# Batch 1's block sums of a pooling layer taken in two rounded passes, with the operands split by ScalarE and GpSimd

## The chip, the cores and the metric

The kernel runs on one core of one Trainium2 chip. The metric is the device time of one execution in microseconds (us). TensorE (PE), VectorE (DVE), ScalarE (ACT), GpSimd (POOL) and SyncE (SP, which issues the DMAs) each take their instructions in program order and wait for one another by semaphores. The program is written by hand, engine by engine, so the order in each of the five streams is the order in the code.

## The reference, cut to what matters

`x` is (2, 1024, 256) in float32. The first layer adds a mixture of eight experts and a shared expert; the second adds a masked softmax pooling over the 1024 positions of each batch:

```python
x = x + _L0_cond_ref(x, ...)             # gated experts, E=8, F=1024, and a shared one
# second layer, hidden = x, A = 64
attn_in = jnp.tanh(jnp.einsum('bsd,da->bsa', hidden, W1) + b1)
scores = jnp.einsum('bsa,a->bs', attn_in, v)
# the mask is l <= j, l >= j or l != j, by the batch's prompt type
masked_scores = jnp.where(mask, scores[:, None, :], -1e30)
p = jax.nn.softmax(masked_scores, axis=-1)
pooled = jnp.einsum('bjl,bld->bjd', p, hidden) / cnt[..., None]
x = x + pooled
```

## The kernel before

The first layer takes nearly all of the time: a loop of 144 groups in which TensorE multiplies split operands. A float32 tensor is split into a rounded part (type fp32r) and what is left (also fp32r), and three matmuls of the parts stand for one float32 matmul. The second layer of batch 0 is woven into the last groups of that loop. The second layer of batch 1, and the pooling of both batches, stand behind the loop, in about the last 27 us.

The pooling works on 8 blocks of 128 positions. Inside a block the masked softmax is a 128x128 matrix `probT` that multiplies the block's rows of `x1` (`pool_probs`, line 1380, plain float32). What a position takes from the other blocks goes through block sums: for each block j the sum of `exp(score - block maximum) * x1` over its 128 positions. `block_sums` (line 1361) makes these with one matrix `e_diag[b][:, j, :]` per block, which holds the weights of block j in column j and in copies of it at 32, 64 and 96, accumulated over the blocks in one PSUM bank, 258 columns wide. ScalarE rounds the sums (`copy_sum`, line 758), VectorE subtracts the rounded part (`rest_sum`, line 1113), and `pool_carries` (line 1388) multiplies them by the carried weights `carry_r` into the same bank as `pool_probs`. `finish` (lines 1122, 1125, 1128) divides and adds, one pair of blocks at a time, into `x_nat`, and SyncE stores each pair. There are four pairs in a batch and four PSUM banks for pooled blocks, so a bank is used again when `finish` has read it (`out_done`).

`e_diag` is made by VectorE in `block_weights`. For batch 0 it is fp32r: three instructions write the rounded weights (line 1097), one forms the rest `e_rest` (line 1102), one writes the rest at column 96 (line 1106). `x1` of batch 0 is split by GpSimd (`split_x1`, lines 617 and 621) while the loop still runs. For batch 1 `e_diag` is plain float32, written by one instruction (line 1091), and `block_sums(1, ...)` multiplies it by the unsplit `x1[1]` in float32.

The order behind the loop, where the change lies:

- TensorE: sums of batch 0, the first four pooled blocks of batch 0, `pick_maxima` (line 1325, batch 1's maxima spread over the lanes), three blocks of batch 1's sums, pooled blocks 4 and 5, the other five blocks of the sums, pooled blocks 6 and 7, then the four pairs of batch 1.
- VectorE: batch 1's maxima (up to line 1061), `block_weights(1)`, `finish` of pair 0, the two arguments of batch 1's exponentials (`prob_args`, line 1081), `finish` of pairs 1 and 2, `rest_sum(1)`, `finish` of pair 3, then `finish` of batch 1.
- ScalarE: the exponential of the block weights (line 754), the eight exponentials of the carried weights (line 770), `round_carry` (779), the exponentials of `probT` (785), with `copy_sum(1)` ahead of the last two.
- GpSimd: waits for `carry_rounded` and takes the rest of each half of `carry_r` (`rest_carry`, line 606).

Of the kernel before, what the change touches and what calls it, by code (L numbers as in the profile page):

```python
# [6 lines left out]
F32 = mybir.dt.float32  # L7
F32R = mybir.dt.float32r
# [5 lines left out]
P = 128  # L14
# [15 lines left out]
NP = 7  # L30


def cond_resid_kernel(nc, x, fside, shared_gate, prompt_type, Wg, Wu, Wd, Sg, Su, Sd, W1, b1, v, out):
# [64 lines left out]
    with ExitStack() as ctx:  # L98
# [4 lines left out]
        def place(name, shape, dt, offset):  # L103
            return nc.alloc_sbuf_tensor_at(name, shape, dt, offset=offset)
# [12 lines left out]
        def sem(name):  # L117
            return ctx.enter_context(nc.semaphore(name))
# [100 lines left out]
        for b in range(B):  # L219
            at = l1_at[b]  # L220
            probT.append(place(f"probT{b}", [P, NJ, P], F32, at))
            at += S * 4

            neg_max.append(place(f"neg_max{b}", [2 * LANE, NJ, P], F32R, at))
            carry_r.append(place(f"carry_r{b}", [P, S], F32R, at))
            at += S * 4
            e_diag.append(place(f"e_diag{b}", [P, NJ, P], F32 if b else F32R, at))
            at += S * 4
            attnT.append(place(f"attnT{b}", [P, BANK], F32, at))
            at += BANK * 4  # L230
            carry.append(place(f"carry{b}", [P, S], F32, at))
            at += S * 4

            for name, where in (("row", row), ("row_self", row_self), ("row_before", row_before),
                                ("row_after", row_after), ("neg", neg)):
                where.append(place(f"{name}{b}", [P, P], F32, at))
                at += P * 4
            neg_r.append(place(f"neg_r{b}", [2 * LANE, P], F32R, at))
            at += P * 4
            x1.append(place(f"x1_{b}", [P, NJ, XA], F32, at))  # L240
            assert at + NJ * XA * 4 <= l1_at[b] + 5 * S * 4 + (NJ * XA * 4 + 511) // 512 * 512 + S * 4


        x1_bytes = (NJ * XA * 4 + 511) // 512 * 512
        assert 2 * x1_bytes <= RAWS * PAIR * (8 * P + D) * 4
        x1_hi = place("x1_hi", [P, NJ, XA], F32R, raw_at)
        x1_lo = place("x1_lo", [P, NJ, XA], F32R, raw_at + x1_bytes)

# [54 lines left out]
        x1_done = sem("x1_done")  # L305
        x1_copied = sem("x1_copied")
        x1_ones = sem("x1_ones")
        x1_rounded = sem("x1_rounded")
        x1_split = sem("x1_split")
        col_done = sem("col_done")  # L310
        col_ready = sem("col_ready")
# [24 lines left out]
        def dve_steps(b, *names):  # L336
            for name in names:
                DVE_L1[name, b] = len(DVE_L1) + 1
# [2 lines left out]
        BLOCKS = ("blkmax", "diag", "before", "after")  # L341
        JOINS = ("bias", "max1", "max2")
        CARRIED = ("carg", "earg", "cmax")
        EDIAG = (("ediag0", "ediag32", "ediag64", "erest", "ediag96"), ("ediag",))
        MAXIMA = ("neg", "negr", "negl", "neg0", "neg1")
        dve_steps(0, *BLOCKS, *CARRIED, *JOINS, *MAXIMA[:4], "parg0", "neg1", "parg1", *EDIAG[0])
        dve_steps(1, *BLOCKS, *JOINS, *CARRIED, *MAXIMA[:3], *EDIAG[1])
        FINISHED = tuple(tuple(f"{n}{j}" for n in ("den", "rden")) for j in range(0, NJ, HEAD))
        dve_steps(0, *FINISHED[0])
        dve_steps(1, "parg0", "parg1")  # L350
        for names in FINISHED[1:]:
            dve_steps(0, *names)
        for names in FINISHED:
            dve_steps(1, *names)
# [101 lines left out]
        def _(pool):  # L456
# [145 lines left out]
            def rest_carry(b, n):  # L602

                half, rows = slice(n * BANK, (n + 1) * BANK), slice(LANES[2], LANES[2] + LANE)
                pool.wait_ge(carry_rounded, b * NT + n + 1)
                nc.gpsimd.tensor_tensor(carry_r[b][rows, half], carry[b][rows, half],
                                        carry_r[b][rows, half].bitcast(F32), ALU.subtract).then_inc(carry_done, 1)

            def split_x1():

                pool.wait_ge(gu_split, NU)
                pool.wait_ge(d_split, NU)
                pool.wait_ge(x1_copied, NB)
                pool.wait_ge(x1_ones, 1)
                for n in range(NB):
                    two = slice(n * JB, (n + 1) * JB)
                    nc.gpsimd.tensor_tensor(x1_hi[:, two, :], x1[0][:, two, :],
                                            zero[:, 0:1].unsqueeze(2).broadcast_to([P, JB, XA]),
                                            ALU.add).then_inc(x1_rounded, 1)
                    pool.wait_ge(x1_rounded, n + 1)  # L620
                    nc.gpsimd.tensor_tensor(x1_lo[:, two, :], x1[0][:, two, :], x1_hi[:, two, :].bitcast(F32),
                                            ALU.subtract).then_inc(x1_split, 1)

            for b in range(B):
                pool.wait_ge(p_done[3], end_of_b[b] + 1)
# [15 lines left out]
            for b in range(B):  # L641
                for n in range(NT):
                    if b * NT + n:
                        pool.wait_ge(carry_done, b * NT + n)
                    rest_carry(b, n)

        @block.scalar
        def _(act):
# [103 lines left out]
            def exp_blocks(b):  # L752
                act.wait_ge(dve_l1, DVE_L1["earg", b])
                nc.scalar.activation(e_blk[:, b, :], e_blk[:, b, :], ACT.Exp).then_inc(e_done, 1)
# [117 lines left out]
            copy_sum(0)  # L872
            copy_x1(1, 2, 3)
            exp_blocks(1)
            halves = [range(n * BANK // P, (n + 1) * BANK // P) for n in range(NT)]
            for blocks in halves:
                exp_carry(1, blocks)
# [8 lines left out]
        def _(dve):  # L886
# [121 lines left out]
            def after_step(name, b):  # L1008
                dve.wait_ge(dve_l1, DVE_L1[name, b])
# [75 lines left out]
            def block_weights(b):  # L1085
                dve.wait_ge(e_done, b + 1)
                dve.wait_ge(diag_zeroed, b + 1)
                e_all = e_blk[:, b, :].unsqueeze(2).broadcast_to([P, NJ, NJ])
                if b:
                    n = len(LANES) - 1  # L1090
                    step_done("ediag", b, nc.vector.tensor_tensor(
                        e_diag[b][:, :, 0:n * LANE].rearrange("p i (n j) -> p i n j", j=LANE)[:, :, :, 0:NJ],
                        e_all.unsqueeze(2).broadcast_to([P, NJ, n, NJ]), eye[:].unsqueeze(2).broadcast_to([P, NJ, n, NJ]),
                        ALU.mult))
                    return
                for at in LANES[:3]:
                    step_done(f"ediag{at}", b, nc.vector.tensor_tensor(e_diag[b][:, :, at:at + NJ], e_all, eye[:],
                                                                       ALU.mult))
                if b == 0:

                    after_step("ediag0", b)
                    step_done("erest", b, nc.vector.tensor_tensor(e_rest[:], e_all, e_diag[b][:, :, 0:NJ].bitcast(F32),
                                                                  ALU.subtract))
                    after_step("erest", b)
                    at = LANES[3]
                    step_done(f"ediag{at}", b, nc.vector.tensor_tensor(e_diag[b][:, :, at:at + NJ], e_rest[:], eye[:],
                                                                       ALU.mult))

            def rest_sum(b):

# [79 lines left out]
            carried_maxima(1)  # L1190
            negative_maxima(1)
            block_weights(1)
            finish(0, range(HEAD))
            for n in range(NT):
                prob_args(1, n)
            finish(0, range(HEAD, 6))
            rest_sum(1)
            finish(0, range(6, NJ))
            finish(1, range(NJ))

        @block.tensor
        def _(pe):
# [147 lines left out]

            def block_sums(b, blocks):
                pe.wait_ge(dve_l1, DVE_L1[EDIAG[b][-1], b])
                if b == 0:
                    pe.wait_ge(x1_split, NB)
                else:
                    pe.wait_ge(x1_copied, NB * (b + 1))
                    pe.wait_ge(x1_ones, b + 1)
                parts = (x1[b],) if b else (x1_hi, x1_lo)
                for j in blocks:
                    for x_part in parts:  # L1360
                        mm = nc.tensor.matmul(SUM[b], e_diag[b][:, j, :], x_part[:, j, :],  # L1361
                                              start=j == 0 and x_part is parts[0],
                                              stop=j == NJ - 1 and x_part is parts[-1], skip_group_check=True)
                if NJ - 1 in blocks:
                    mm.then_inc(sum_done, 1)

# [115 lines left out]
            pick_maxima(0)  # L1482
            pe.wait_ge(dve_l1, DVE_L1["earg", 1])
            pick_maxima(1)
            block_sums(1, range(3))
            pool_probs(0, range(4, 6))
            pool_carries(0, range(4, 6))
            block_sums(1, range(3, NJ))
            pool_probs(0, range(6, NJ))
            pool_carries(0, range(6, NJ))  # L1490
            for j in range(0, NJ, HEAD):
                pool_probs(1, range(j, j + HEAD))
                pool_carries(1, range(j, j + HEAD))
# [21 lines left out]
```

## Time and profile before

| | |
|---|---|
| median of 3 runs | 1130.52 us (1130.36 to 1130.83) |
| the profiled execution, its own time | 1130.71 us |
| its span in the trace | 1129.0 us |
| TensorE busy | 1121.3 us, 99% of the span |
| VectorE busy | 796.2 us, 71% |
| ScalarE busy | 650.8 us, 58% |
| GpSimd busy | 288.9 us, 26% |

The time is 1.7 us longer than the span, since it also holds what lies before the first and behind the last traced instruction. TensorE's 99% is the share of an instruction being in flight. Behind the loop the engines take turns, and there the order of waits counts more than the shares.

### The profile page before, as it was taken

What the parts mean: (1) busy time and instruction counts of PE and PEld (TensorE: products, weight loads), DVE (VectorE), ACT (ScalarE), POOL (GpSimd) and SP (SyncE); (2) the same over time, 40 slices, a digit from 0 to 9 for tenths busy, and PEclk for the clock granted to TensorE, in tenths of its full rate; (3) what the DMA queues carried; (4) which work ended last, traced back from release to release, by engine and by line L of the source; (5) the groups of instructions that cost most, each with busy time, mean ns of one, the idle gap of its engine ahead of it and who ended that gap; (6) DMA issues with size and microseconds to landing.
All of it is one profiled execution on the core that took longest, in us unless ns stands there. A gap on an engine that the chain in (4) does not pass through costs nothing.

```text
span 1129.0 us, 14925 instructions
## 1 busy us (share of the span) xinstructions
PE 1121.3 (99%) x4961; PEld 922.7 (82%) x4961; DVE 796.2 (71%) x1163; ACT 650.8 (58%) x1170; POOL 288.9 (26%) x378
## 2 busy tenths in 40 slices
PE   8999999999999999999999999999999999999998
PEld 6788888888888888888888888888888888887886
DVE  7977777667677766667667767677777777666866
ACT  7756655555555555555555555555555556555654
POOL 7611612133241202021211111111212034301441
PEclk9999999999999999999999999999999999999999
DMA  5200110000000000000000000000000011100002
GB/s 161 71 15 29 48 31 10 26 28 28 29 28 29 29 29 28 29 28 28 29 28 29 29 17 13 29 28 29 29 28 29 28 43 42 57 1 29 1 1 75
DMA packets 38637, 36.70 MB, mean 33 GB/s; under 512 B 3232, under 2 KB 38560, under 8 KB 38560
## 3 DMA queue, kind: packets, MB, share of 16 engines
q1 hardware_dynamic: 37744, 35.21, 9.7%
q8 instruction: 40, 0.66, 0.2%
q10 hardware_dynamic: 816, 0.52, 0.2%
q14 instruction: 37, 0.30, 0.1%
HBM read 33.63 MB, written 2.10 MB: 32 GB/s over the span
## 4 chain that ended last, share of the span: by engine, by line
PE 96%; DVE 1%; DVEq 0%; issue 0%
PE acc_of L1220 12%; PE acc_of L1222 11%; PE acc_of L1221 11%; PE v_both L1220 8%; PE v_both L1222 8%; PE v_both L1221 8%; PE e_ps L1221 6%; PE e_ps L1222 6%; PE e_ps L1220 6%; PE g_ps L1222 6%; PE g_ps L1221 6%; PE g_ps L1220 6%; PE e_ps L1295 1%; DVE x_nat L1128 0%; PE g_ps L1361 0%; PE v_both L1361 0%
## 5 line engine op out<-in xcount | busy, mean ns | idle before, releaser
L1220 PE MATMUL acc_of<-h_hi,wd_hi 128*128 128x512 f32 x576 | 225.6, 392 | 0.0
L1222 PE MATMUL acc_of<-h_lo,wd_hi 128*128 128x512 f32 x576 | 224.5, 390 | 0.0
L1221 PE MATMUL acc_of<-h_hi,wd_lo 128*128 128x512 f32 x576 | 224.4, 390 | 0.0
L697 ACT ACTIVATE silu<-g_ps 128x512 f32<-128x512 f32 x144 | 86.2, 599 | 223.8 <-PE g_ps L1222 223.8
L691 ACT ACTIVATE v_both<-g_ps 128x512 f32<-128x512 f32 x144 | 83.8, 582 | 189.4 <-PE g_ps L1222 187.8
L964 DVE TENSOR_TENSOR gate<-e_ps,v_part 128x512 f32<-128x512 f32 x144 | 99.5, 691 | 118.0 <-PE e_ps L1222 117.8
L984 DVE SCALAR_TENSOR_TENSOR v_both<-silu,gates,v_both 128x512 f32<-128x512 f32 x144 | 108.7, 755 | 92.6 <-PE v_both L1222 91.5
L1220 PE MATMUL v_both<-xs_hi,wq_hi 128*128 128x512 f32 x432 | 168.7, 391 | 0.8 <-DVE up L969 0.5
L1222 PE MATMUL v_both<-xs_lo,wq_hi 128*128 128x512 f32 x432 | 168.3, 390 | 0.0
L1221 PE MATMUL v_both<-xs_hi,wq_lo 128*128 128x512 f32 x432 | 168.3, 390 | 0.0
L496 POOL TENSOR_TENSOR wd_hi<-raw_d,zero 128x256 fp32r<-128x256 f32 x80 | 55.1, 689 | 419.2 <-PE acc_of L1222 417.2
L485 POOL TENSOR_TENSOR raw<-raw 128x512 f32<-128x512 f32 (+1 forms) x41 | 54.4, 1326 | 358.2 <-DMA raw<-in_L_cond_Wu 318.7
L989 DVE TENSOR_TENSOR h_lo<-v_both,h_hi 128x512 fp32r<-128x512 f32 x144 | 99.6, 692 | 48.8 <-ACT h_hi L721 48.4
L969 DVE TENSOR_TENSOR up<-v_both,p_sb 128x512 f32<-128x512 f32 x144 | 98.8, 686 | 41.8 <-PE v_both L1222 41.7
L1220 PEld LDWEIGHTS acc_of<-h_hi,wd_hi 128*128 128x128 f32 x576 | 108.2, 188 | 23.0 <-issue 0.7
L1221 PEld LDWEIGHTS acc_of<-h_hi,wd_lo 128*128 128x128 f32 x576 | 108.2, 188 | 22.3 <-issue 0.2
L1222 PEld LDWEIGHTS acc_of<-h_lo,wd_hi 128*128 128x128 f32 x576 | 108.2, 188 | 22.4
L978 DVE SCALAR_TENSOR_TENSOR h<-silu,gates,up 128x512 f32<-128x512 f32 x144 | 116.1, 806 | 11.4 <-POOL gates L579 0.6
L1220 PE MATMUL e_ps<-xs_hi,wq_hi 128*128 128x512 f32 x288 | 112.5, 391 | 1.2 <-POOL wq_lo L480 0.7
L1220 PE MATMUL g_ps<-xs_hi,wq_hi 128*128 128x512 f32 x288 | 112.6, 391 | 0.4 <-ACT v_both L691 0.4
L1221 PE MATMUL e_ps<-xs_hi,wq_lo 128*128 128x512 f32 x288 | 112.2, 390 | 0.0
L1222 PE MATMUL e_ps<-xs_lo,wq_hi 128*128 128x512 f32 x288 | 112.2, 390 | 0.0
(199 smaller groups left out, 1920.4 us busy)
## 6 DMA issues: line engine op xcount, KB each, us to landing
raw_d<-in_L_cond_Wd SPq DMA_DIRECT2D x35, 256.0 KB, 3.7
raw<-in_L_cond_Wg SPq DMA_DIRECT2D x34, 256.0 KB, 2.6
raw<-in_L_cond_Wu SPq DMA_DIRECT2D x34, 256.0 KB, 3.2
out_x<-x_nat SPq DMA_DIRECT2D x8, 256.0 KB, 2.2
x_nat<-in_x SPq DMA_DIRECT2D x7, 256.0 KB, 5.1
raw<-in_L_cond_Sg SPq DMA_DIRECT2D x5, 256.0 KB, 2.6
raw<-in_L_cond_Su SPq DMA_DIRECT2D x5, 256.0 KB, 3.0
raw_d<-in_L_cond_Sd SPq DMA_DIRECT2D x5, 256.0 KB, 3.6
```

Source lines behind the costliest of these rows:

```text
L485: t_made(nc.gpsimd.tensor_tensor(w[:, 4:6, :], w[:, 1:4:2, :], w[:, 0:1, :].broadcast_to([P, 2, n]), ALU.subtract))
L496: nc.gpsimd.tensor_tensor(wd_hi[:, n % RING, :], raw_d[:, s, j, :], zero[:, 0:1].broadcast_to([P, D]), ALU.add).then_inc(d_hi_done, 1)
L691: nc.scalar.activation(v_ps[i % 2][:], g_ps[:], ACT.Copy).then_inc(seeded, 1)
L697: nc.scalar.activation(silu0[:, i % 2, :], g_ps[:], ACT.Silu).then_inc(silu0_done, 1)
L964: nc.vector.tensor_tensor(gate1[:], e_ps[:], v_part[:], ALU.add).then_inc(gate1_done, 1)
L969: nc.vector.tensor_tensor(up1[:], v_ps[i % 2][:], p7_sb[:], ALU.add).then_inc(up1_done, 1)
L978: nc.vector.scalar_tensor_tensor(out=h1[:], in0=silu1[:], scalar=gate_of(i), in1=up1[:], op0=ALU.mult, op1=ALU.mult).then_inc(h_done[1], 1)
L984: nc.vector.scalar_tensor_tensor(out=v_ps[i % 2][:], in0=silu0[:, i % 2, :], scalar=gate_of(i), in1=v_ps[i % 2][:], op0=ALU.mult, op1=ALU. ...
L989: nc.vector.tensor_tensor(h_lo[t][:, i % HB, :], h_of(t, i), h_hi[t][:, i % HB, :].bitcast(F32), ALU.subtract).then_inc(h_split[t], 1)
L1220: nc.tensor.matmul(ps, w_hi, a_hi, start=start, stop=False, skip_group_check=True)
L1221: nc.tensor.matmul(ps, w_lo, a_hi, start=False, stop=False, skip_group_check=True)
L1222: return nc.tensor.matmul(ps, w_hi, a_lo, start=False, stop=stop, skip_group_check=True)
```

## The change

Batch 1's block sums become what batch 0's are: two fp32r matmuls a block, of the rounded and the remaining part of `x1[1]`, with an fp32r `e_diag`. ScalarE rounds `x1[1]` in four instructions between the exponential of the block weights and those of the carried weights. GpSimd takes the four rests (`rest_x1`) between batch 0's and batch 1's `rest_carry`. VectorE's `block_weights(1)` has two more instructions. TensorE takes the sums in two halves of four blocks, behind pooled blocks 4 and 5 and behind 6 and 7, and waits for the rests two blocks at a time. VectorE finishes pair 1 ahead of `prob_args`, and `rest_sum(1)` comes behind pair 3. The split of `x1[1]` lies where the weights of the first layer were.

```diff
-        x1_hi = place("x1_hi", [P, NJ, XA], F32R, raw_at)
-        x1_lo = place("x1_lo", [P, NJ, XA], F32R, raw_at + x1_bytes)
+        x1_at = (raw_at, wq_at + pick_bytes)
+        x1_hi = [place(f"x1_hi{b}", [P, NJ, XA], F32R, at) for b, at in enumerate(x1_at)]
+        x1_lo = [place(f"x1_lo{b}", [P, NJ, XA], F32R, at + x1_bytes) for b, at in enumerate(x1_at)]
...
+            def rest_x1(b, n):
+
+                two = slice(n * JB, (n + 1) * JB)
+                pool.wait_ge(x1_rounded[b], n + 1)
+                nc.gpsimd.tensor_tensor(x1_lo[b][:, two, :], x1[b][:, two, :], x1_hi[b][:, two, :].bitcast(F32),
+                                        ALU.subtract).then_inc(x1_split, 1)
...
                     rest_carry(b, n)
+                if b == 0:
+                    pool.wait_ge(carry_done, NT)
+                    for n in range(NB):
+                        rest_x1(1, n)
+                    pool.wait_ge(x1_split, B * NB)
...
             exp_blocks(1)
+            act.wait_ge(p_done[3], NG)
+            act.wait_ge(x1_ones, B)
+            act.wait_ge(x1_copied, B * NB)
+            for n in range(NB):
+                two = slice(n * JB, (n + 1) * JB)
+                nc.scalar.activation(x1_hi[1][:, two, :], x1[1][:, two, :], ACT.Copy).then_inc(x1_rounded[1], 1)
...
-                    return
-                for at in LANES[:3]:
...
+                    after_step("ediag", b)
+                else:
+                    for at in LANES[:3]:
...
+                step_done("erest", b, nc.vector.tensor_tensor(e_rest[:], e_all, e_diag[b][:, :, 0:NJ].bitcast(F32),
+                                                              ALU.subtract))
+                after_step("erest", b)
+                at = LANES[3]
+                step_done(f"ediag{at}", b, nc.vector.tensor_tensor(e_diag[b][:, :, at:at + NJ], e_rest[:], eye[:],
+                                                                   ALU.mult))
...
-            finish(0, range(HEAD))
+            finish(0, range(2 * HEAD))
             for n in range(NT):
                 prob_args(1, n)
-            finish(0, range(HEAD, 6))
+            finish(0, range(2 * HEAD, NJ))
             rest_sum(1)
-            finish(0, range(6, NJ))
             finish(1, range(NJ))
...
                 for j in blocks:
-                    for x_part in parts:
+                    if j % JB == 0:
+                        pe.wait_ge(x1_split, b * NB + j // JB + 1)
+                    for x_part in (x1_hi[b], x1_lo[b]):
...
-            block_sums(1, range(3))
             pool_probs(0, range(4, 6))
             pool_carries(0, range(4, 6))
-            block_sums(1, range(3, NJ))
+            block_sums(1, range(4))
             pool_probs(0, range(6, NJ))
             pool_carries(0, range(6, NJ))
+            block_sums(1, range(4, NJ))
```

## Rows read from the trace of the kernel before

**Rows 1.** The page: busy time by engine, and TensorE's clock in 40 slices.

```profile
PE 1121.3 (99%) x4961; PEld 922.7 (82%) x4961; DVE 796.2 (71%) x1163; ACT 650.8 (58%) x1170; POOL 288.9 (26%) x378
...
PEclk9999999999999999999999999999999999999999
```

**Rows 2.** The chain that ended last: start and length in us, engine, tile, line.

```profile
1108.55 1.43 PE v_both L1361 x12
...
1113.54 1.03 PE acc_of L1325 x8
1114.57 1.50 PE g_ps L1361 x6
...
1117.18 2.18 PE g_ps L1361 x10
1119.36 0.87 PE v_both L1380 x4
1120.23 0.25 PE v_both L1388 x2
...
1120.51 0.17 DVE den L1122
```

**Rows 3.** Timeline of ScalarE behind the loop: start and length, us.

```profile
1100.76 1.13 ACT L779 ACTIVATE carry_r<-carry 128x512 fp32r<-128x512 f32 x2
...
1111.89 0.21 ACT L754 ACTIVATE e_blk<-e_blk 128x8 f32<-128x8 f32 x1
1114.22 2.17 ACT L770 ACTIVATE carry<-acc_of,carry_bias 128x128 f32<-128x128 f32 x8 [2.12 <-PE acc_of L1325]
```

**Rows 4.** Timeline of VectorE behind the loop.

```profile
1104.41 0.21 DVE L1102 TENSOR_TENSOR e_rest<-e_blk,e_diag 128x64 f32<-128x64 f32 x1
1104.66 0.23 DVE L1106 TENSOR_TENSOR e_diag<-e_rest,eye 128x64 fp32r<-128x64 f32 x1
...
1112.62 0.28 DVE L1061 TENSOR_TENSOR neg_r<-neg,neg_r 32x128 fp32r<-32x128 f32 x1
1112.93 0.36 DVE L1091 TENSOR_TENSOR e_diag<-e_blk,eye 128x192 f32<-128x192 f32 x1
1113.21 0.15 DVE L1122 TENSOR_TENSOR den<-acc_of,cnt 128x2 f32<-128x2 f32 x1
...
1116.85 0.69 DVE L1081 TENSOR_TENSOR probT<-acc_of,mask 128x512 f32<-128x512 f32 x1 [0.69 <-ACT carry L770]
1117.45 0.15 DVE L1122 TENSOR_TENSOR den<-v_both,cnt 128x2 f32<-128x2 f32 x1
...
1118.63 0.15 DVE L1122 TENSOR_TENSOR den<-acc_of,cnt 128x2 f32<-128x2 f32 x1
```

**Rows 5.** One line of GpSimd: shortest, median and longest in ns.

```profile
L621 POOL TENSOR_TENSOR x_lo<-x,x_hi x4: 1288/1638/1643, 1072.1 to 1080.4; 128x516 fp32r<-128x516 f32 x4
```

**Rows 6.** Timelines of GpSimd and VectorE, 1101.5 to 1104.3 us.

```profile
1101.51 2.62 POOL L606 TENSOR_TENSOR carry_r<-carry,carry_r 32x512 fp32r<-32x512 f32 x2 [2.82 <-ACT carry_r L779]
...
1103.53 0.69 DVE L1097 TENSOR_TENSOR e_diag<-e_blk,eye 128x64 fp32r<-128x64 f32 x1
```

**Rows 7.** Line 1097, its three instructions: shortest, median, longest in ns.

```profile
L1097 DVE TENSOR_TENSOR e_diag<-e_blk,eye x3: 211/214/689, 1103.5 to 1104.3; 128x64 fp32r<-128x64 f32 x3
```

**Rows 8.** Timelines of GpSimd and VectorE in the loop, 58 to 61 us.

```profile
58.03 1.30 POOL L485 TENSOR_TENSOR raw<-raw 128x512 f32<-128x512 f32 x1 [7.21 <-DMA raw<-in_L_cond_Wu]
58.60 1.28 DVE L916 TENSOR_TENSOR xs_lo<-xT,xs_hi 128x512 fp32r<-128x512 f32 x1
59.41 1.06 POOL L487 TENSOR_TENSOR raw<-raw 128x256 f32<-128x256 f32 x1
59.80 1.22 DVE L916 TENSOR_TENSOR xs_lo<-s_tmp,xs_hi 128x512 fp32r<-128x512 f32 x1
```

**Rows 9.** Timeline of TensorE: its first matmuls, and one behind an early gap.

```profile
1.52 3.35 PE L1217 MATMUL v_both<-blank 128*128 128x512 f32 x7 [1.52 <-DVE blank L887]
...
12.23 0.50 PE L1220 MATMUL e_ps<-xs_hi,wq_hi 128*128 128x512 f32 x1 [0.67 <-POOL wq_lo L480]
```

More of the change, by code:

```diff
@@ L226, in cond_resid_kernel @@
             at += S * 4
-            e_diag.append(place(f"e_diag{b}", [P, NJ, P], F32 if b else F32R, at))
+            e_diag.append(place(f"e_diag{b}", [P, NJ, P], F32R, at))
             at += S * 4
@@ L245, in cond_resid_kernel @@
         assert 2 * x1_bytes <= RAWS * PAIR * (8 * P + D) * 4
-        x1_hi = place("x1_hi", [P, NJ, XA], F32R, raw_at)
-        x1_lo = place("x1_lo", [P, NJ, XA], F32R, raw_at + x1_bytes)
+        pick_bytes = NJ * P * 4
+        assert pick_bytes + 2 * x1_bytes <= RING * NP * P * 4
+        x1_at = (raw_at, wq_at + pick_bytes)
+        x1_hi = [place(f"x1_hi{b}", [P, NJ, XA], F32R, at) for b, at in enumerate(x1_at)]
+        x1_lo = [place(f"x1_lo{b}", [P, NJ, XA], F32R, at + x1_bytes) for b, at in enumerate(x1_at)]
         pick = place("pick", [2 * LANE, NJ, P], F32R, wq_at)
@@ L307, in cond_resid_kernel @@
         x1_ones = sem("x1_ones")
-        x1_rounded = sem("x1_rounded")
+        x1_rounded = [sem(f"x1_rounded{b}") for b in range(B)]
         x1_split = sem("x1_split")
@@ L343, in cond_resid_kernel @@
         CARRIED = ("carg", "earg", "cmax")
-        EDIAG = (("ediag0", "ediag32", "ediag64", "erest", "ediag96"), ("ediag",))
+        EDIAG = (("ediag0", "ediag32", "ediag64", "erest", "ediag96"), ("ediag", "erest", "ediag96"))
         MAXIMA = ("neg", "negr", "negl", "neg0", "neg1")
@@ L348, in cond_resid_kernel @@
         FINISHED = tuple(tuple(f"{n}{j}" for n in ("den", "rden")) for j in range(0, NJ, HEAD))
-        dve_steps(0, *FINISHED[0])
+        for names in FINISHED[:2]:
+            dve_steps(0, *names)
         dve_steps(1, "parg0", "parg1")
-        for names in FINISHED[1:]:
+        for names in FINISHED[2:]:
             dve_steps(0, *names)
@@ L616, in split_x1 @@
                     two = slice(n * JB, (n + 1) * JB)
-                    nc.gpsimd.tensor_tensor(x1_hi[:, two, :], x1[0][:, two, :],
+                    nc.gpsimd.tensor_tensor(x1_hi[0][:, two, :], x1[0][:, two, :],
                                             zero[:, 0:1].unsqueeze(2).broadcast_to([P, JB, XA]),
[L619 to L622, printed above, removed]
+                                            ALU.add).then_inc(x1_rounded[0], 1)
+                    rest_x1(0, n)
+            def rest_x1(b, n):
[3 more added lines that the diff above has]
+                                        ALU.subtract).then_inc(x1_split, 1)
             for b in range(B):
@@ L1094, in block_weights @@
                         ALU.mult))
-                    return
-                for at in LANES[:3]:
-                    step_done(f"ediag{at}", b, nc.vector.tensor_tensor(e_diag[b][:, :, at:at + NJ], e_all, eye[:],
-                                                                       ALU.mult))
-                if b == 0:
-                    after_step("ediag0", b)
[L1102 to L1107, printed above, removed]
+                    after_step("ediag", b)
+                else:
+                    for at in LANES[:3]:
+                        step_done(f"ediag{at}", b, nc.vector.tensor_tensor(e_diag[b][:, :, at:at + NJ], e_all, eye[:],
+                                                                           ALU.mult))
+                    after_step("ediag0", b)
+                step_done("erest", b, nc.vector.tensor_tensor(e_rest[:], e_all, e_diag[b][:, :, 0:NJ].bitcast(F32),
[3 more added lines that the diff above has]
+                step_done(f"ediag{at}", b, nc.vector.tensor_tensor(e_diag[b][:, :, at:at + NJ], e_rest[:], eye[:],
+                                                                   ALU.mult))
             def rest_sum(b):
@@ L1352, in block_sums @@
                 pe.wait_ge(dve_l1, DVE_L1[EDIAG[b][-1], b])
[L1353 to L1358, printed above, removed]
                 for j in blocks:
-                    for x_part in parts:
+                    if j % JB == 0:
+                        pe.wait_ge(x1_split, b * NB + j // JB + 1)
+                    for x_part in (x1_hi[b], x1_lo[b]):
                         mm = nc.tensor.matmul(SUM[b], e_diag[b][:, j, :], x_part[:, j, :],
-                                              start=j == 0 and x_part is parts[0],
-                                              stop=j == NJ - 1 and x_part is parts[-1], skip_group_check=True)
+                                              start=j == 0 and x_part is x1_hi[b],
+                                              stop=j == NJ - 1 and x_part is x1_lo[b], skip_group_check=True)
                 if NJ - 1 in blocks:
```

## The prediction

> **What bounds the kernel now.** I read the page first. TensorE has an instruction in flight for 99% of the span, at the granted clock of nine tenths or more in every slice [rows 1], so the loop is bound by TensorE; but the change touches nothing of the loop. The chain that ended last shows what sets the end behind it. The reader is to see that until 1120.48 it runs through TensorE without a break: `pick_maxima`, then three blocks of batch 1's sums (1.50 us), pooled blocks 4 and 5, five blocks of sums (2.18 us), pooled blocks 6 and 7 [rows 2]. From 1120.51 it is VectorE's, one pair of `finish` after another. A pair takes 1.18 us (1117.45 to 1118.63 [rows 4]), so batch 1's first pair begins at 1120.51 + 1.18 = 1121.69. Four pairs and the last store follow it. I call that start X: these pairs stay as they are, and the change is worth what it moves X. TensorE's part of a later pair is 0.87 + 0.25 = 1.12 us [rows 2], a little under 1.18, so VectorE goes on setting the pace.
>
> Then I read the timelines of ScalarE, VectorE and GpSimd from 1111.8 on. ScalarE idles 2.12 us ahead of line 770 [rows 3]. VectorE idles before `prob_args`, since it waits for ScalarE [rows 4]. So both seem to have room for the added work. The last thing I looked for is what VectorE and GpSimd do to each other when both work, since the change puts GpSimd work beside VectorE's.
>
> **TensorE's sums.** Before, 8 blocks cost 1.50 + 2.18 = 3.68 us in float32. In two rounded passes, twelve matmuls of batch 0's took 1.43 us, 0.12 each [rows 2], so 16 cost 1.9 us. That is 1.8 us less on TensorE. It counts only while TensorE sets X.
>
> **ScalarE.** Two instructions of line 779 on the same shape took 1.13 us, 0.52 apart [rows 3]. Four rounding instructions behind line 754, from 1112.01 on, start at 1112.01, 1112.53, 1113.05 and 1113.57 and are done at 1114.2. Line 770 began at 1114.22 when it had waited for TensorE [rows 3]. The 2.1 us lie in the idle time: cost 0 to 0.1, taken as 0. Without that cover they would delay line 770 by 2.1.
>
> **VectorE, if nothing disturbs it.** `block_weights(1)` gains 0.21 and 0.23 us [rows 4] and two waits: 0.5 us. Pair 0 then starts at 1113.71 instead of 1113.21, pair 1 follows at 1114.9, `prob_args` at 1116.1 and 1116.7, pair 2 at 1117.3, pair 3 at 1118.5, `rest_sum` at 1119.7. Its 0.42 us end at 1120.1; TensorE's first carries and the way there and back I put at 0.6 (two matmuls from a standing start, some 0.5, and the hand-overs; bounds 0.4 and 0.8). X would be 1120.7: a gain of 1.0 us. The saved 1.8 us is not reached, because VectorE then has no idle time left.
>
> **The collision.** GpSimd's rests start when ScalarE has rounded. Line 606 began 0.75 us after line 779 had begun [rows 3, 6], so the first rest of `x1[1]` is ready at 1112.01 + 0.75 = 1112.76; with the added waits I take 1112.8. VectorE is then in line 1061, until 1112.90, and line 1091 would begin at 1112.93 [rows 4]. All of 1091, 1102 and 1106 read two SBUF tensors. The rows show what this means. The same step for batch 0, line 1097, took 0.69 us where its shortest took 0.211 [rows 6, 7]: GpSimd's line 606 had the time from 1101.51 to 1104.13, and VectorE's instruction ended at 1104.22, 0.09 behind it. It could not run beside it. And in the loop they alternate: GpSimd to 1059.33, VectorE's line 916 ended at 1059.88; GpSimd's line 487 started at 1059.41 but was served behind that; and VectorE's next, right behind the first, was served behind 487, which ended at 1060.47 [rows 8]. So VectorE does not keep its turn between two of its own instructions.
>
> The Trainium skill says as much in "SBUF — State Buffer", section "SBUF: two separate sides": the port pair that VectorE and GpSimd share is an exclusive lock for a whole instruction, against a VectorE instruction with two SBUF inputs too. The trace agrees, by the 0.48 us that line 1097 lost. By that rule the loss is as in the sum below; without it, the forecast would be the gain of 1.0.
>
> The shortest rest took 1.288 us, the others 1.64, beside VectorE work [rows 5]. I go by 1.29 plus the wait for VectorE. Step by step:
>
> - Rest 0 comes at 1112.8, begins behind line 1061 and ends at 1114.15. Line 1091 waits for it and ends at 1114.4 (1.1 us late).
> - Rest 1 has come at 1114.1, is served behind line 1091, and ends at 1115.5. Line 1102 waits, and ends at 1115.6.
> - Rest 2 came at 1115.5 and ends at 1116.8. Line 1106 waits, and ends at 1116.85. Rest 3 ends at 1118.0.
>
> Pair 0 has one SBUF tensor and one in PSUM, and starts at 1116.8, 3.6 us later than before. Line 606 for batch 1 goes from 1118.0 to 1119.3, and is not late.
>
> **What is late next.** Pooled blocks 4 and 5 use pair 0's banks. TensorE, done with `pick_maxima` at 1114.57 [rows 2], stands for 3.1 us, until the first half of pair 0 is written, at 1117.65. Then come blocks 4 and 5 (done 1118.8), sums of blocks 0 to 3 (1119.8), blocks 6 and 7 (1120.9), the rest of the sums (1121.9). VectorE has pair 1 at 1118.0, `prob_args` at 1119.2 and 1119.8 (0.60 from one to the next, as 1116.85 to 1117.45 [rows 4]), pair 2 at 1120.4, pair 3 at 1121.6, `rest_sum` at 1122.75. ScalarE's exponentials of `probT` start behind `prob_args`; with `round_carry` they leave `copy_sum` from 1122.2 to 1122.6, just in time. `rest_sum` ends at 1123.2, and X is 1123.8: 2.1 us later than 1121.7.
>
> The bounds of the unknown parts: the order at line 1091 (next part, worth 1.1), the way there and back (0.4 to 0.8), a rest at 1.2 to 1.4 us without the wait (three of them: 0.3 either way). The gates for the output stores move with the pairs and keep their distance, so they cost nothing; `e_diag` in fp32r costs what it did. TensorE's added waits for the rests cost nothing, since all but the last rest are there when asked for, and the last sums start after 1120.
>
> **The sum.** The profiled execution took 1130.71 us, 0.19 above the median of 1130.52. Its 1130.71 + 2.1 is 1132.8; against the median I forecast 1132.6 us.
>
> **The rivals.**
>
> A, the forecast: three rests each come ahead of one VectorE instruction. 1132.6, own range 1131.9 to 1133.4. Chance 0.55.
>
> B: the first rest comes after 1112.93, so that line 1091 goes first. For it: only 0.13 us lie between the two, and ScalarE has three more waits to take. Then rest 0 ends at 1114.45, line 1102 at 1114.5, rest 1 at 1115.7, line 1106 at 1115.8; pair 0 starts 1.1 us earlier than in A. 1131.5, range 1131.0 to 1132.0. Chance 0.2.
>
> C: VectorE is not held up, because the rests come only behind line 1106 (1113.8) or VectorE keeps its turn. Then X is 1120.7 and the time 1129.5. Against it stand rows 6 to 8. Chance 0.07.
>
> D, clearly slower: TensorE's clock falls in the 3.1 us in which A lets it stand. No row behind the start has such a gap; the one of 0.67 us did no harm to speak of (0.50 us for the matmul behind it), but the first seven matmuls, behind idle time, took 0.48 us each [rows 9]. At half the rate, pooled blocks 4 and 5 and four blocks of sums take 4.1 us instead of 2.05, of which 0.4 are slack: 1.7 us more, 1134.3. If the clock stays low, a pair costs TensorE 2.24 us against 1.18, and four pairs add 4 more: up to 1139. It decides from the point where the clock falls ahead of 1117.65. Chance 0.13.
>
> The Trainium skill, "TensorE: Matmul & The Clock Gate", Part 1, has the clock fall to 1.2 GHz behind idle time. No row here shows it fall, so it stays a rival.
>
> The remaining 0.05 is for what I don't see.
>
> **How the numbers follow.** The likeliest is A, 1132.6. The range 1130.9 to 1134.3 holds B and A and the mildest of D; C, most of D and the unseen, together under 0.2, are left out. What a measurement can tell from no change is about 0.2%, 2.3 us: below 1128.3 or above 1132.8. A lies just inside, and passes it in some 4 of 10 cases: 0.21, with D's 0.13 and 0.01 of the unseen 0.35 for slower. B, C and the rest of A are within: 0.63. Faster by that much would take more than C gives: 0.02.
>
> **What the profile of the changed kernel would show.** Lines of the changed file have moved, so I go by tiles. The `e_diag` instruction of 128x192, the `e_rest` and the 128x64 one behind it should last over 1 us each, where 0.36, 0.21 and 0.23 are their own times; the four `x_lo` of batch 1 should run back to back from 1112.8. TensorE's first matmul behind `pick_maxima` should be idle before it for 3 us on VectorE's `x_nat`. If instead these three last 0.2 to 0.4 us, it is C; if only the first is short, B. If the matmuls behind the gap are 0.12 us apart in the sums, the clock held. ScalarE's line for `carry` should still wait for TensorE. I would be wrong if GpSimd's rests came late, or if `rest_sum` waited for ScalarE instead of following pair 3.

## The result and the profile after

The changed kernel took 1134.11 us, median of 7 runs (1134.07 to 1135.37), against 1130.68 us for the kernel before beside it. The ratio is 1.0034, with an interval of 1.0025 to 1.0044: slower, by 3.4 us at the median. Its runs lie at two levels: four at 1134.1 and three at 1135.1 to 1135.4. The profiled execution is of the upper level: 1135.37 us, span 1133.7, which is 4.7 longer than the span before. The median lies inside the forecast's range of 1130.9 to 1134.3, at its upper end; the likeliest value was 1132.6, and most of the chance (0.63) lay on a change too small to tell from none.

Where it went shows in three timelines of the changed kernel. In all of them 0.2 us must be taken off before they are compared with rows of before, since the loop ended that much later in this execution (`attn(1)` began at 1102.52 instead of 1102.31). First VectorE, with start, length and, in brackets, the idle time before and who ended it:

```profile
1112.83 0.28 DVE L1083 TENSOR_TENSOR neg_r<-neg,neg_r 32x128 fp32r<-32x128 f32 x1
1113.14 1.45 DVE L1113 TENSOR_TENSOR e_diag<-e_blk,eye 128x192 fp32r<-128x192 f32 x1
1114.63 1.18 DVE L1124 TENSOR_TENSOR e_rest<-e_blk,e_diag 128x64 f32<-128x64 f32 x1
1115.84 1.20 DVE L1128 TENSOR_TENSOR e_diag<-e_rest,eye 128x64 fp32r<-128x64 f32 x1
1116.96 0.15 DVE L1144 TENSOR_TENSOR den<-acc_of,cnt 128x2 f32<-128x2 f32 x1
...
1119.31 1.28 DVE L1103 TENSOR_TENSOR probT<-acc_of,mask 128x512 f32<-128x512 f32 x2
...
1123.96 0.16 DVE L1144 TENSOR_TENSOR den<-v_both,cnt 128x2 f32<-128x2 f32 x1 [2.20 <-PE v_both L1405]
...
1125.33 0.42 DVE L1135 TENSOR_TENSOR blk_sum<-g_ps,blk_sum 32x258 fp32r<-32x258 f32 x1
1126.35 0.16 DVE L1144 TENSOR_TENSOR den<-acc_of,cnt 128x2 f32<-128x2 f32 x1 [0.59 <-PE acc_of L1405]
```

The three instructions of `block_weights` take 1.45, 1.18 and 1.20 us; 0.36, 0.21 and 0.23 are their times undisturbed [rows 4]. GpSimd has its four rests in the same 5 us:

```profile
1113.09 5.09 POOL L631 TENSOR_TENSOR x_lo<-x,x_hi 128x516 fp32r<-128x516 f32 x4 [8.75 <-ACT x_hi L896]
1118.26 1.26 POOL L611 TENSOR_TENSOR carry_r<-carry,carry_r 32x512 fp32r<-32x512 f32 x1
```

And TensorE, behind the spread of the maxima:

```profile
1113.66 1.11 PE L1346 MATMUL acc_of<-neg_r,pick 64*128 64x128 f32 x8
1117.88 2.09 PE L1397 MATMUL acc_of<-x,probT 128*128 128x258 f32 x4 [3.11 <-DVE x_nat L1150]
1119.41 0.99 PE L1405 MATMUL acc_of<-blk_sum,carry_r 128*128 128x258 f32 x2
1120.20 0.42 PE L1378 MATMUL g_ps<-x_hi,e_diag 128*128 128x258 f32 x1
1120.41 0.42 PE L1378 MATMUL g_ps<-x_lo,e_diag 128*128 128x258 f32 x1
...
1123.76 0.28 PE L1378 MATMUL g_ps<-x_hi,e_diag 128*128 128x258 f32 x1
1123.88 0.28 PE L1378 MATMUL g_ps<-x_lo,e_diag 128*128 128x258 f32 x1
```

It stands for 3.11 us, and then the sums come 0.21 us apart in the first half and 0.12 apart in the second. The changed kernel's windows say why. The columns are the window, its length, the busy time and instructions of TensorE, its weight loads, VectorE, ScalarE and GpSimd, the granted clock as a share of 2.4 GHz, and the DMA's share and GB/s:

```profile
1114.50:1116.50 2.00, 0.27 (x3) 0.13 (x2) 1.93 (x3) 2.00 (x10) 2.00 (x2) 1.00 0.00 0
1116.50:1117.90 1.40, 0.02 (x1) 0.02 (x1) 1.33 (x5) 0.62 (x2) 1.40 (x2) 0.53 0.00 0
1117.90:1122.80 4.90, 4.90 (x17) 4.34 (x18) 3.73 (x11) 2.38 (x7) 2.32 (x3) 0.50 0.34 117
1122.80:1130.00 7.20, 6.98 (x37) 5.69 (x35) 5.06 (x18) 0.96 (x3) 0.48 (x1) 0.96 0.34 118
```

The clock fell to 0.50, the level of 1.2 GHz, while TensorE stood, and it stayed there through the next 4.9 us of work. The means of the second and the last window place the fall at about 1116.6, inside the gap, and the return at about 1123.4. So the forecast's chain of waits is there, and rival D, the fall of the clock, came on top of it. Batch 1's first pair started at 1126.35, which is 1126.1 on the clock of before, 4.4 us behind 1121.7.

### The profile page after: what moved, and what is told of

It is laid out like the page before. It is cut to its first block, busy times and chain, and to the rows that moved or that the text cites. A ratio compares the mean times of both kernels' runs of the same rounds, so it can differ in the third digit from the quotient of the medians.

```text
span 1133.7 us, 14937 instructions
## 1 busy us (share of the span) xinstructions
PE 1123.0 (99%) x4961; PEld 923.4 (81%) x4961; DVE 797.6 (70%) x1165; ACT 653.2 (58%) x1174; POOL 295.2 (26%) x382
## 4 chain that ended last, share of the span: by engine, by line
PE 95%; DVE 1%; issue 0%; ACT 0%; DVEq 0%; ACTq 0%
PE acc_of L1241 11%; PE acc_of L1242 11%; PE acc_of L1243 11%; PE v_both L1241 8%; PE v_both L1242 8%; PE v_both L1243 8%; PE e_ps L1241 6%; PE e_ps L1242 6%; PE e_ps L1243 6%; PE g_ps L1241 6%; PE g_ps L1242 6%; PE g_ps L1243 6%; PE e_ps L1316 1%; DVE x_nat L1150 0%; PE g_ps L1378 0%
## 5 line engine op out<-in xcount | busy, mean ns | idle before, releaser
L1243 PE MATMUL g_ps<-xs_lo,wq_hi 128*128 128x512 f32 x288 | 112.1, 389 | 0.0
```

The costliest lines, as they stand in the source:

```text
L1243: return nc.tensor.matmul(ps, w_hi, a_lo, start=False, stop=stop, skip_group_check=True)
```

## The experiments

Eight runs of seven kernels, each timed in five rounds beside the kernel before. The first four ran on one chip beside 1130.54 us for the kernel before, the next two beside 1130.77, the last two beside 1130.73.

**e1_fill12: the clock held up by other work.** Twelve matmuls that nothing reads go into the gap of the changed kernel:

```diff
             pick_maxima(1)
+            pe.wait_ge(x1_copied, B * NB)
+            for k in range(12):
+                nc.tensor.matmul(g_ps[:], h_hi[0][:, 0, 0:P], h_hi[1][:, 0, :], start=True, stop=True)
```

> The changed kernel with 12 matmuls of 512 columns into the free sums bank behind the spread of the maxima, about 2.6 us of TensorE work in the 3.1 us gap; they add nothing to the output. Theory 1 (three waits of VectorE behind GpSimd cost about 2.1 us, and the lower clock behind the gap the other 1.4 to 2.6): granted clock 1.00 throughout, the 16 sum matmuls 0.12 us apart, pair 0 still at 1117.0, time 2.1 us over the kernel before, 1132.7. Rival (the clock costs nothing because TensorE has slack; the late pairs alone set the end): time as of the changed kernel, 3.4 us or more over before.

Measured: 1132.70 us (1132.61 to 1133.0, 11 runs, one level), 2.16 over the kernel before; ratio 1.0020, interval 1.0011 to 1.0029. Two timelines of this kernel, VectorE's and TensorE's:

```profile
1112.82 1.46 DVE L1113 TENSOR_TENSOR e_diag<-e_blk,eye 128x192 fp32r<-128x192 f32 x1
1114.31 1.21 DVE L1124 TENSOR_TENSOR e_rest<-e_blk,e_diag 128x64 f32<-128x64 f32 x1
1115.55 1.22 DVE L1128 TENSOR_TENSOR e_diag<-e_rest,eye 128x64 fp32r<-128x64 f32 x1
1116.69 0.15 DVE L1144 TENSOR_TENSOR den<-acc_of,cnt 128x2 f32<-128x2 f32 x1
...
1122.72 0.42 DVE L1135 TENSOR_TENSOR blk_sum<-g_ps,blk_sum 32x258 fp32r<-32x258 f32 x1
1123.73 0.16 DVE L1144 TENSOR_TENSOR den<-acc_of,cnt 128x2 f32<-128x2 f32 x1 [0.59 <-PE acc_of L1405]
```

```profile
1114.38 2.99 PE L1504 MATMUL g_ps<-h_hi,h_hi 128*128 128x512 f32 x12
1117.62 1.14 PE L1397 MATMUL acc_of<-x,probT 128*128 128x258 f32 x4 [0.24 <-DVE x_nat L1150]
...
1118.83 0.28 PE L1378 MATMUL g_ps<-x_hi,e_diag 128*128 128x258 f32 x1
1118.95 0.28 PE L1378 MATMUL g_ps<-x_lo,e_diag 128*128 128x258 f32 x1
```

VectorE is as late as in the changed kernel; TensorE has the same work from 1117.6 on, but its clock is full. Each against its own runs of the kernel before, the changed kernel is 3.4 us slower at its lower level and 4.6 at its upper one (1135.2), and this one is 2.2 slower. So the clock cost 1.3 us at the lower level and 2.4 at the upper. The forecast's case A has become real here. The loop ended 0.1 us earlier in this execution than in that of before; with 0.1 added, pair 0 is at 1116.8 (forecast 1116.8), `rest_sum` at 1122.8 (1122.75), and batch 1's first pair at 1123.8 (1123.8).

**e2_rests_late: the collision taken away.** GpSimd starts its rests only when `block_weights(1)` is done:

```diff
                     pool.wait_ge(carry_done, NT)
+                    pool.wait_ge(dve_l1, DVE_L1[EDIAG[1][-1], 1])
                     for n in range(NB):
                         rest_x1(1, n)
```

> The changed kernel with one more wait on GpSimd: the first rest of batch 1 starts only behind VectorE's last e_diag instruction. Theory 1: the three VectorE instructions take 0.36, 0.21 and 0.23 us, pair 0 starts 0.5 us later than before the change, TensorE has no gap over 0.3 us, the clock holds, the rests run from about 1114.2 to 1119.2, and the first pair of batch 1 starts at about 1121.1: 0.6 us faster than the kernel before (range 0.2 to 1.1). Rival (the two-pass sums and their new place cost time by themselves, or the late rests hold up the last sums and the carried rest): no faster than before, up to 2 us slower.

Measured: 1130.13 us (1130.07 to 1130.36), 0.41 under the kernel before; ratio 0.9997, interval 0.9988 to 1.0005. Against the kernel before, one wait has turned 3.4 us more into 0.4 less: 3.8 us. The gain over the kernel before is not shown, since the interval holds 1, though all of its runs lie under the median of before. In the profile batch 1's first pair is 0.4 us earlier than before, when the 0.2 are added by which this loop ended earlier. VectorE's timeline in this kernel, and one line of TensorE's:

```profile
1112.75 0.36 DVE L1114 TENSOR_TENSOR e_diag<-e_blk,eye 128x192 fp32r<-128x192 f32 x1
1113.14 0.22 DVE L1125 TENSOR_TENSOR e_rest<-e_blk,e_diag 128x64 f32<-128x64 f32 x1
1113.40 0.23 DVE L1129 TENSOR_TENSOR e_diag<-e_rest,eye 128x64 fp32r<-128x64 f32 x1
...
1120.07 0.42 DVE L1136 TENSOR_TENSOR blk_sum<-g_ps,blk_sum 32x258 fp32r<-32x258 f32 x1 [0.54 <-ACT blk_sum L774]
1121.08 0.16 DVE L1145 TENSOR_TENSOR den<-acc_of,cnt 128x2 f32<-128x2 f32 x1 [0.59 <-PE acc_of L1406]
```

```profile
1118.87 0.39 PE L1379 MATMUL g_ps<-x_hi,e_diag 128*128 128x258 f32 x1 [0.19 <-POOL x_lo L631]
```

The three instructions have their own times again. Rests that start late end late: the last one at 1118.8, the last sums behind it, and `rest_sum` waits 0.54 us for their rounding. That wait is about what is missing from the 1.0 us that case C of the prediction gave.

**e3_rests_mid and e8_mid_again: half the collision, and a gap of 1 us.** GpSimd waits for the first `e_diag` instruction only. The same kernel ran twice, each time beside the kernel before:

```diff
                     pool.wait_ge(carry_done, NT)
+                    pool.wait_ge(dve_l1, DVE_L1["ediag", 1])
```

> The changed kernel with one more wait on GpSimd: the first rest of batch 1 starts only behind VectorE's first e_diag instruction (128x192). Theory 1 (strict turns): e_rest still goes ahead of the first rest, the last e_diag instruction waits for it and takes about 1.2 us, pair 0 starts 1.6 us later than before, TensorE stands for 1.1 us and keeps its clock; time within 0.5 us of the kernel before. Rival (VectorE loses to GpSimd at each of its two remaining instructions): pair 0 2.5 us later, a gap of 2 us, time 1 us or more over before.

> The variant in which the rests wait for the first e_diag instruction, once more and without filler matmuls: is the share of executions at the upper level a matter of the execution? Theory 1 (the clock falls in some executions, in others not): two levels again, most near 1132 and some at 1130.5 to 1130.8. Rival (the lower level came from elsewhere): one level near 1132.

Measured: 1131.99 us (ratio 1.0010, 1.0001 to 1.0019) and 1130.98 us (ratio 1.0005, 0.9996 to 1.0014). In the first, three runs lie at 1130.5 to 1130.8 and eight at 1131.9 to 1132.2; in the second, seven at 1130.6 to 1131.0 and four at 1132.4 to 1132.6. The collision came as expected: `e_rest` went ahead (0.23 us), the last `e_diag` instruction took 1.20. But the time did not, in most of the first eleven runs: their median is 1.45 us over the kernel before, and I had expected the clock to hold through a gap of 1 us. The two profiles happened to be of the two levels. The first, in its windows and TensorE's timeline:

```profile
1114.50:1115.70 1.20, 0.15 (x3) 0.04 (x1) 1.13 (x5) 1.20 (x6) 1.20 (x2) 1.00 0.00 0
1115.70:1119.20 3.50, 3.50 (x13) 3.13 (x14) 3.36 (x11) 2.59 (x9) 3.42 (x4) 0.53 0.44 150
```

```profile
1115.66 1.87 PE L1398 MATMUL acc_of<-x,probT 128*128 128x258 f32 x4 [1.05 <-DVE x_nat L1151]
```

The second, in the same views:

```profile
1114.50:1115.70 1.20, 0.13 (x3) 0.01 (x1) 1.13 (x5) 1.20 (x6) 1.20 (x2) 1.00 0.00 0
1115.70:1119.20 3.50, 3.50 (x22) 3.23 (x23) 3.36 (x11) 2.57 (x9) 3.42 (x4) 1.00 0.42 150
```

```profile
1115.70 1.14 PE L1398 MATMUL acc_of<-x,probT 128*128 128x258 f32 x4 [1.07 <-DVE x_nat L1151]
```

The gap is the same, 1.05 and 1.07 us; in one execution the clock fell just behind it and 13 matmul records fit into the 3.5 us, in the other it held and 22 fit. The executions' own times are 1132.18 and 1130.96. The other twenty have no trace, but each run on record has its mean granted clock: it is 0.998 in all twelve executions of the upper level and 0.999 or 1.000 in all ten of the lower. So the two levels go with the clock in every one of the 22. In the changed kernel the same number is 0.998 in the four executions of its lower level and 0.997 in the three of its upper.

**e5_mid_fill4: the same with four filler matmuls.** e3, with filler as in e1:

```diff
             pick_maxima(1)
+            pe.wait_ge(x1_copied, B * NB)
+            for k in range(4):
+                nc.tensor.matmul(g_ps[:], h_hi[0][:, 0, 0:P], h_hi[1][:, 0, :], start=True, stop=True)
```

> The variant in which the rests wait for the first e_diag instruction, with 4 matmuls of 512 columns in TensorE's gap of 1.05 us. That variant ran at two levels, 1130.5 to 1130.8 in three executions and 1131.9 to 1132.2 in eight, and its profile shows the granted clock at half from 1115.8 to 1119.1. Theory 1 (the upper level is the one with the clock fall): all executions at the lower level, 1130.4 to 1130.9, clock 1.00. Rival (the two levels come from elsewhere, as from the output stores or GpSimd's turns): two levels again, median near 1132.

Measured: 1130.94 us (1130.48 to 1131.35, 11 runs), ratio 1.0002 (0.9993 to 1.0011), the profiled one with clock 1.0. The runs spread more than I had expected, as did those of the kernel before beside them (1130.40 to 1131.12), but none of the eleven is at the level near 1132, where 12 of 22 without the filler were, and none has a mean clock under 0.999. So the upper level is the clock's.

**e4_split_only: the added work beside the kernel before.** ScalarE's four rounding instructions and GpSimd's four rests are put into the kernel before, into tensors that nothing reads:

```diff
                     rest_carry(b, n)
+                if b == 0:
+                    pool.wait_ge(carry_done, NT)
+                    for n in range(NB):
+                        two = slice(n * JB, (n + 1) * JB)
+                        pool.wait_ge(x1b_rounded, n + 1)
+                        nc.gpsimd.tensor_tensor(x1b_lo[:, two, :], x1[1][:, two, :], x1b_hi[:, two, :].bitcast(F32),
+                                                ALU.subtract).then_inc(x1b_split, 1)
+                    pool.wait_ge(x1b_split, NB)
...
             exp_blocks(1)
...
+            for n in range(NB):
+                two = slice(n * JB, (n + 1) * JB)
+                nc.scalar.activation(x1b_hi[:, two, :], x1[1][:, two, :], ACT.Copy).then_inc(x1b_rounded, 1)
```

> The kernel before, with the added work of ScalarE and GpSimd alone: batch 1's operand is rounded and its rests are taken at the same places, into tensors that nothing reads; sums, VectorE and TensorE stay as before. Theory 1: the one e_diag instruction waits for the first rest and takes 1.4 us, pair 0 starts 1.1 us later, but TensorE asks for its bank only at 1116, so the time is that of the kernel before within 0.2 us. Rival (GpSimd's occupation of the shared port by itself costs what the change costs, at any VectorE instruction): 1 us or more over before.

Measured: 1130.56 us (1130.45 to 1130.78), ratio 1.0000 (0.9991 to 1.0009). VectorE's timeline:

```profile
1112.83 1.46 DVE L1109 TENSOR_TENSOR e_diag<-e_blk,eye 128x192 f32<-128x192 f32 x1
1114.21 0.15 DVE L1140 TENSOR_TENSOR den<-acc_of,cnt 128x2 f32<-128x2 f32 x1
```

A collision of 1.1 us is there, and costs nothing: pair 0 is 1.1 us late (1114.21, where everything stands 0.1 earlier than before), but TensorE has sums to do and asks for pair 0's bank 1.4 us after `pick_maxima`. In the changed order it asks at once, and three instructions wait instead of one.

**e6_first_early: the first rest taken ahead.** e2, with the first of the four rounded right behind its copy and rested while VectorE still waits for the scores. The diff is against the changed kernel:

```diff
                     pool.wait_ge(carry_done, NT)
-                    for n in range(NB):
+                    rest_x1(1, 0)
+                    pool.wait_ge(dve_l1, DVE_L1[EDIAG[1][-1], 1])
+                    for n in range(1, NB):
                         rest_x1(1, n)
...
             copy_x1(1, 0)
...
+            act.wait_ge(x1_copied, NB + 1)
+            nc.scalar.activation(x1_hi[1][:, 0:JB, :], x1[1][:, 0:JB, :], ACT.Copy).then_inc(x1_rounded[1], 1)
...
-            for n in range(NB):
+            for n in range(1, NB):
```

> The variant in which the rests wait for VectorE's last e_diag instruction, with the first of the four rounded and rested ahead, while VectorE waits for the scores (ScalarE rounds it right behind its copy). There VectorE waited 0.54 us for ScalarE's rounded sums, which waited for the last rest. Theory 1: the other three rests end at 1117.6 instead of 1118.8, that wait goes, the batch 1 pairs start 0.5 us earlier; 1129.6, 0.9 us under the kernel before. Rival (the early rounding holds up the scores' columns on ScalarE, or the early rest the maxima on VectorE): the gain is given back ahead of 1112, time 1130.1 or more.

Measured: 1129.91 us (1129.59 to 1130.18) against 1130.77 (1130.40 to 1131.12): 0.86 under the kernel before, ratio 0.9992 (0.9983 to 1.0001). The two sets of runs do not overlap, but the interval just holds 1, so the gain is likely and not shown. VectorE's timeline:

```profile
1119.74 0.42 DVE L1139 TENSOR_TENSOR blk_sum<-g_ps,blk_sum 32x258 fp32r<-32x258 f32 x1
1120.76 0.16 DVE L1148 TENSOR_TENSOR den<-acc_of,cnt 128x2 f32<-128x2 f32 x1 [0.60 <-PE acc_of L1409]
```

`rest_sum` no longer waits, and batch 1's first pair is at 1120.76, against 1121.70 before.

**e7_sums_ahead: `rest_sum` ahead of pair 3.** e6, with all eight blocks of the sums in one piece, and ScalarE's rounding of them and `rest_sum` moved ahead. The diff is against e6:

```diff
+            copy_sum(1)
             round_carry(1, 1)
             exp_probs(1, halves[1][:HEAD])
-            copy_sum(1)
...
-            finish(0, range(2 * HEAD, NJ))
+            finish(0, range(2 * HEAD, 6))
             rest_sum(1)
+            finish(0, range(6, NJ))
...
-            block_sums(1, range(4))
+            block_sums(1, range(NJ))
             pool_probs(0, range(6, NJ))
             pool_carries(0, range(6, NJ))
-            block_sums(1, range(4, NJ))
```

> The variant with the first rest early and the others behind the last e_diag instruction, with all eight blocks of batch 1's sums ahead of pooled blocks 6 and 7, ScalarE's rounding of the sums ahead of its second round_carry, and VectorE's rest_sum ahead of pair 3. There VectorE stood for 0.6 us between rest_sum and batch 1's first pair, with pair 3 already done. Theory 1: pair 3 now fills that time; the sums are done at 1118.0, rest_sum ends at 1118.9, and batch 1's first pair starts at 1120.3 to 1120.5 instead of 1120.8: 0.3 to 0.5 us under that variant, 1129.5. Rival (TensorE sets the pace, since pooled blocks 6 and 7 come 1 us later and everything behind them too): no gain, 1129.9 or more.

Measured: 1130.05 us (1129.79 to 1130.37), ratio 0.9994 (0.9985 to 1.0003), 0.68 under the kernel before, where e6 was 0.86 under: no gain over e6. TensorE waits inside the sums for the last rest, and pair 3 then waits for TensorE, as the rival had it; batch 1's first pair is at 1120.77, as in e6. TensorE's timeline, and VectorE's:

```profile
1117.70 0.39 PE L1383 MATMUL g_ps<-x_hi,e_diag 128*128 128x258 f32 x1 [0.25 <-POOL x_lo L631]
```

```profile
1118.89 0.42 DVE L1139 TENSOR_TENSOR blk_sum<-g_ps,blk_sum 32x258 fp32r<-32x258 f32 x1 [0.39 <-ACT blk_sum L775]
1119.58 0.16 DVE L1148 TENSOR_TENSOR den<-v_both,cnt 128x2 f32<-128x2 f32 x1 [0.27 <-PE v_both L1410]
...
1120.77 0.15 DVE L1148 TENSOR_TENSOR den<-acc_of,cnt 128x2 f32<-128x2 f32 x1
```

## Why the prediction was wrong

**What held.** The collision, in place and in size: the order of turns at all three instructions, pair 0 at 1116.8 (1116.96 in the changed kernel less 0.2), the gap of 3.1 us (3.11). So is the sum of 2.1 us for it, which e1 measured at 2.16 by itself. The order at the first instruction was closer than the forecast had it, though: the rounding began 0.1 us later than 1112.01, and in the profiles of the changed kernel, e1 and e4 the first rest stands only 0.04 to 0.05 us ahead of the `e_diag` instruction, where the forecast gave 0.13. That case B, worth 1.1 us less, did not come instead was in part luck. ScalarE's work fitted into its idle time: 1112.32 to 1114.5, with the exponentials of the carried weights at 1114.43, 0.0 later than before when 0.2 are taken off. The two-pass sums are 0.12 us a matmul at the full clock. The reason to expect a gain without the collision held in part: by the medians, e2 gives 0.4 of the 1.0. Case C put the rests behind line 1106, at 1113.8, but did not follow them further: four of 1.27 us end at 1118.8 in e2's profile, and the sums wait for the last. e6 gives 0.86. One reading was written down wrong, without effect: the four times given from rows 8 as 1059.33 to 1060.47 are 59.33 to 60.47 us, early in the loop.

**What failed.** The step "TensorE stands for 3.1 us" carried no price in the sum: TensorE was taken to go on at full rate behind the gap, and the fall of the clock was left a rival at a chance of 0.13. It was the case that came, and it cost 1.3 us at the lower level and 2.4 at the upper (e1). The reasons given against it were that no row shows the clock fall, though no row behind the start has such a gap either, and the gap of 0.67 us [rows 9], which is a fifth of the gap in question and so says little. The better sign stood in the same rows: the first seven matmuls took 0.48 us each behind idle time, and in e1 twelve of the same shape took 2.99 us together, 0.25 each, at full clock. (The granted clock reads 1.00 at the start too, so the durations are the only sign there.) The price worked out for the rival, 1.7 us and 1134.3 in all, lies between the two levels; that the median of 1134.11 comes so near to it is in part luck. The upper level comes about as the prediction says: pooled blocks 4 and 5 and four blocks of sums take 4.0 us (forecast 4.1), and pair 3 waits 2.20 us. But the low clock also takes in most of pooled blocks 6 and 7, which took 1.8 us from their first matmul to the next sums, where e1 has 1.1; the price did not count these 0.7, and 1.7 and 0.7 are the 2.4 of the upper level. The executions at the lower level were not profiled. Their mean clock of 0.998 gives, by an estimate, 3 to 6 us at the lower clock (a mean of 0.998 lacks 0.0015 to 0.0025; twice that share of a span of 1132 us), against 6.8 in the profiled one (1116.6 to 1123.4). So the clock was low for less time in them; whether it fell later or came back sooner stays open.

**How it was shown.** Filler matmuls take away the clock's fall and leave VectorE's three long instructions and pair 0 where they were (e1); the late rests take away the collision, the gap and the fall together (e2); the same program at the same gap runs at both levels, with a full clock in one profile and half in the other (e3, e8) and a lower mean clock in every execution of the upper level, and it runs at the lower alone with filler work (e5). That the collision alone is harmless where TensorE has other work is e4.

## What to carry to other kernels

When work is moved to GpSimd, list VectorE's instructions with two SBUF inputs that fall in the same stretch: each lost 1.0 to 1.1 us here beside GpSimd instructions of 1.26 to 1.38 us, and consecutive ones lost it each. A wait that makes GpSimd start behind them returned 3.8 us on balance, clock included, though it made the rests end late enough to hold up `rest_sum` by 0.54 us; taking the first rest earlier, while VectorE waited for the scores, removed that too (e6). And when a change makes TensorE stand, even for 1 us, a fall of the clock belongs in the sum with a chance of its own, priced as the next few microseconds of its work at half rate; either leave it other work there or take the gap away.

## What the runs showed of the hardware

- TensorE's clock fell behind a gap of 1.05 us in a stretch in which TensorE had been busy throughout, in 12 of 22 executions of one program (e3, e8: mean clock 0.998 against 0.999 or 1.000, one profile of each kind), and not in the others; with four filler matmuls in that gap it fell in none of 11 (e5); behind 3.11 us all seven executions of the changed kernel are 1.2 us or more over what e1 adds to the kernel before, with mean clocks of 0.997 or 0.998 where all of e1's are 0.999 or 1.000, and the one profiled shows the fall.
- In the profile of e3 the granted clock was still 1.00 through the gap and fell to half when TensorE already worked again (0.53 in the mean over 1115.7 to 1119.2). In that of the changed kernel it fell inside the gap, at about 1116.6.
- VectorE and GpSimd took turns instruction by instruction: VectorE's instructions of 0.21 and 0.23 us, with two SBUF inputs, took 1.18 and 1.20 between GpSimd's rests, and 1.21 and 1.22 in e1. At both, GpSimd's next rest went ahead of VectorE's next instruction. VectorE's instructions with one operand in PSUM ran at their own times beside the same rests: `den` in 0.15 us while the fourth rest ran.
